# Quantised groups in pieces, constant matrix products in other places, and five quantisations one slot later, in a two-layer transformer kernel

## The reference

```python
# layer 0
h = layernorm(x) * (1 + ca) + sa
Qr, Kr = rotate(h @ Wq.T), rotate(h @ Wk.T)
x = x + ga * softmax(where(mask, Qr @ Kr.T / sqrt(128), -inf)) @ (h @ Wv.T)
h = layernorm(x) * (1 + cb) + sb
gate, y = fp4(h) @ fp4(w_gate).T, fp4(h) @ fp4(w_up).T          # 352 columns
x = x + gb * (fp4(silu(gate) * y) @ fp4(w_down).T)
# layer 1, other rows of modulation
h = layernorm(x) * (1 + ca) + sa
x = x + ga * softmax(causal(h @ qk @ h.T / sqrt(128))) @ h @ ov
h = layernorm(x) * (1 + cb) + sb
x = x + gb * (top2_experts(h) + shared_expert(h))
```

## Time and profile before

| | us |
|---|---|
| median of three runs | 714.09 (713.89 to 716.97) |
| the profiled execution | 714.27 |
| its span, from the first to the last instruction | 712.4 |
| TensorE busy in matrix products | 625.6 (88%), 3764 instructions |
| VectorE busy | 479.4 (67%), 1270 |
| ScalarE busy | 339.9 (48%), 693 |
| GpSimd busy | 226.1 (32%), 248 |
| granted TensorE clock, mean over the span | 0.978 |

### The profile page before, as it was taken

One profiled execution on the slowest core, in us unless ns is written; L12 is line 12 of the kernel. 1 busy time (PEld: TensorE's weight loads), 2 busy tenths in 40 slices (PEclk: granted clock), 3 DMA queues, 4 the chain that ended last, 5 costly groups with the idle time before them and its releaser, 6 DMA issues.

```text
span 712.4 us, 10866 instructions
## 1 busy us (share of the span) xinstructions
PE 625.6 (88%) x3764; PEld 486.2 (68%) x3782; DVE 479.4 (67%) x1270; ACT 339.9 (48%) x693; POOL 226.1 (32%) x248
## 2 busy tenths in 40 slices
PE   5888898988779989988899889868889996998996
PEld 4356687877556778775678777746668874676774
DVE  5966499786777557627569886687545436775665
ACT  1133454565535464443445465534655553554553
POOL 3424645453644301005456454474310002000000
PEclk9989999999999999999999999989999999999999
DMA  8200000000000000000000000100000000001011
GB/s 248 81 1 1 1 2 1 1 1 1 1 0 1 2 1 1 1 2 1 1 1 1 1 1 1 52 5 1 1 1 1 1 1 1 0 16 29 16 30 30
DMA packets 12173, 9.64 MB, mean 14 GB/s; under 512 B 1804, under 2 KB 10840, under 8 KB 12120
## 3 DMA queue, kind: packets, MB, share of 16 engines
q1 hardware_dynamic: 12120, 8.95, 4.2%
HBM read 6.84 MB, written 2.10 MB: 13 GB/s over the span
## 4 chain that ended last, share of the span: by engine, by line
PE 58%; DVE 21%; ACT 8%; POOL 7%; issue 5%; DMA 1%; SPq 0%; ACTq 0%; POOLq 0%; DVEq 0%
PE ps L819 12%; PE ps L687 10%; PE ps L797 7%; PE ps L968 4%; PE ps L970 4%; PE ps L969 4%; PE ps L646 3%; ACT xn L1087 2%; PE ps L842 2%; PE ps L707 2%; PE ps L843 2%; POOL rstd L516 2%; PE ps L858 2%; DVE row_max L1410 1%; DVE ha L1455 1%
## 5 line engine op out<-in xcount | busy, mean ns | idle before, releaser
L1147 ACT ACTIVATE probsT<-ps 128x512 f32<-128x512 f32 (+3 forms) x160 | 85.2, 533 | 162.8 <-PE ps L797 162.8
L819 PE MATMUL ps<-v_sb,probsT 128*128 128x129 f32 (+1 forms) x1124 | 151.4, 279 | 3.7 <-ACT probsT L1149 3.7
L819 PEld LDWEIGHTS ps<-v_sb,probsT 128*128 128x128 f32 (+1 forms) x1124 | 137.6, 191 | 8.8 <-ACT probsT L1149 5.5
L1410 DVE TENSOR_REDUCE row_max<-ps 128x1 f32<-128x512 f32 (+2 forms) x144 | 87.7, 620 | 54.4 <-PE ps L687 25.7
L797 PE MATMUL ps<-ident,probs 128*128 128x128 f32 (+1 forms) x562 | 90.8, 278 | 15.2 <-ACT hT L1077 7.8
L1121 ACT ACTIVATE probs<-ps,neg_max 128x512 f32<-128x512 f32 (+7 forms) x158 | 93.1, 620 | 17.9 <-DVE neg_max L1417 14.1
L797 PEld LDWEIGHTS ps<-ident,probs 128*128 128x128 f32 (+1 forms) x562 | 64.4, 140 | 46.0 <-issue 42.1
L545 POOL TENSOR_TENSOR hq<-ha,hp 128x352 f32<-128x352 f32 x32 | 29.9, 934 | 118.3 <-DVE hp L1460 118.3
L1222 ACT ACTIVATE probs<-ps 128x512 f32<-128x512 f32 x40 | 24.0, 599 | 44.8 <-PE ps L970 44.8
L687 PE MATMUL ps<-k_high,q_high 128*128 128x512 f32 (+5 forms) x100 | 42.1, 421 | 2.8 <-ACT probs L1121 2.2
L515 POOL TENSOR_SCALAR minus_mean<-mv 128x4 f32<-128x4 f32 (+1 forms) x16 | 3.8, 238 | 122.7 <-DVE veps L1278 122.5
(11 more groups left out here) (245 smaller groups left out, 1372.7 us busy)
## 6 DMA issues: line engine op xcount, KB each, us to landing
out<-x_sb SPq DMA_DIRECT2D x8, 256.0 KB, 2.3
x_sb<-in_L_attn_x SPq DMA_DIRECT2D x2, 512.0 KB, 6.5
hT_all<-in_L_wmod SPq DMA_DIRECT2D x2, 384.0 KB
rope_cos<-table_cos SPq DMA_DIRECT2D x1, 768.0 KB, 8.1
rope_sin<-table_sin SPq DMA_DIRECT2D x1, 768.0 KB, 10.1
rope_cos<-table_cos SPq DMA_DIRECT2D x1, 256.0 KB, 4.5
rope_sin<-table_sin SPq DMA_DIRECT2D x1, 256.0 KB, 6.2
moe_raw<-in_L_ffn_expert_gate_w SPq DMA_DIRECT2D x1, 256.0 KB, 2.7
```

The source lines that it names most:

```text
L819: mm = pe.matmul(bank(OUT_AT, 0, V_W), probsT[0:size, n % 4, k * P:(k + 1) * P], v_sb[0:size, j, :], start=(c == 0 and k == 0), stop=(c == ...
L1147: ins = act.activation(probsT[:, n % 4, 0:full], bank(TURN, 0, full), ACT.Copy)
L1410: ins = dve.tensor_reduce(dst, ps[:, start:start + width], AX.X, ALU.max, negate=single)
```

## The change

- `modulate_1` works tile by tile: eight instructions of 128 columns for two of 512, and ScalarE signals every normalised tile.
- `xq_scaled`, the transposition and the copy of a group work in two parts (`FP4_PARTS`): the first tile, then the other three. TensorE transposes the first tile in slot 4g + 6 and the others in slot 4g + 7.
- `grid_slot(n)` is the slot in which tile n is quantised: n + 6 as before, but n + 7 for tiles 10 to 14 (`GRID_LATE`). Of these, 10 to 13 are quantised by VectorE ahead of the next tile's gating, and 14 at tile 15's place, ahead of it. The transposition of these tiles stays where it was.
- The constant products in `WAITS_AT_HEAD` go. New are some inside `turn_group`, behind the wait for the bank and ahead of the wait for the input (`WAITED_FOR`: 3 for norm0's groups 1 to 3; 2, 8, 10 and 5 for norm2's four), three ahead of each of the keys' projections in slots 0, 2 and 4, 11 or 18 for the 9 at the end of a batch and 4 behind them, and 10 ahead of the sums over the experts' choices. In batch 0 that is 20 products more, in batch 1 27 more.
- From slot 4 on the rounding of rotated keys and queries stands at the end of a slot on ScalarE (L1156) and behind `modulate_1` and `hq_scaled` on GpSimd (L575).

```diff
 SLOTS = 2 * TILES
+FP4_PARTS = ((0, 1), (1, GROUP))
 FFN_LAG, DOWN_LAG = 6, 8
-
-
-WAITS_AT_HEAD = {FFN_LAG: 11, TILES + 1: 8, TILES + 5: 10}
+GRID_LATE = range(TILES - FFN_LAG, TILES - 1)
+
+
+WAITED_FOR = {**{("norm0", g): 3 for g in range(1, GROUPS)}, ("norm2", 0): 2, ("norm2", 1): 8, ("norm2", 2): 10, ("norm2", 3): 5}
+
+
+def grid_slot(n):
+
+    return n + FFN_LAG + (n in GRID_LATE)
 
...
-    firsts = (("fp4_in", FFN_LAG), ("norm2", DOWN_LAG + GROUP + 1), ("norm3", TILES + GROUP + 2))
+    firsts = (("fp4_first", FFN_LAG), ("fp4_rest", FFN_LAG + 1), ("norm2", DOWN_LAG + GROUP + 1), ("norm3", TILES + GROUP + 2))
     turns = [(kind, group_at(slot, first)) for kind, first in firsts if group_at(slot, first) is not None]
...
-                    pool.wait_ge(h_step, b * 2 * GROUPS + 2 * g + 1)
-                    pool.tensor_tensor(h, h, row(0), ALU.add).then_inc(h_step, 1)
+                    tiles = [xn[:, g, t * P:(t + 1) * P] for t in range(GROUP)]
+                    first = b * TILES + g * GROUP
+
+                    def add_shift(t):
+                        pool.wait_ge(h_scaled, first + t + 1)
+                        pool.tensor_tensor(tiles[t], tiles[t], mod_row_now[:, 0, :], ALU.add).then_inc(h_shifted, 1)
+
+                    for t in range(GROUP):
+                        pool.wait_ge(xn1_ready, first + t + 1)
+                        pool.tensor_tensor(tiles[t], tiles[t], mod_row_now[:, 1, :], ALU.mult).then_inc(h_scaled, 1)
+                        if t:
+                            add_shift(t - 1)
+                    add_shift(GROUP - 1)
...
-                    pool.tensor_tensor(xq[:], qa[:], qp[:], ALU.add).then_inc(xq_step, 1)
-                    pool.wait_ge(xq_step, b * 2 * GROUPS + 2 * g + 1)
-                    pool.tensor_tensor(xq[:], xq[:], qp[:], ALU.subtract).then_inc(xq_step, 1)
-                    pool.wait_ge(xq_step, b * 2 * GROUPS + 2 * g + 2)
-                    blocks = xq[:].rearrange("p (k e) -> p k e", e=BLOCK)
-                    pool.tensor_tensor(blocks, blocks, qs[:, 2, :].unsqueeze(2).to_broadcast(
-                        [P, GROUP * P // BLOCK, BLOCK]), ALU.mult).then_inc(xq_ready, 1)
+                        pool.wait_ge(turned, TURN_AT[b, "fp4_rest", g - 1] + 1)
+                    for part, (a, z) in enumerate(FP4_PARTS):
+                        cols, done = slice(a * P, z * P), b * 4 * GROUPS + 4 * g + 2 * part
+                        pool.tensor_tensor(xq[:, cols], qa[:, cols], qp[:, cols], ALU.add).then_inc(xq_step, 1)
+                        pool.wait_ge(xq_step, done + 1)
+                        pool.tensor_tensor(xq[:, cols], xq[:, cols], qp[:, cols], ALU.subtract).then_inc(xq_step, 1)
+                        pool.wait_ge(xq_step, done + 2)
+                        by_block = xq[:, cols].rearrange("p (k e) -> p k e", e=BLOCK)
+                        scales = qs[:, 2, a * P // BLOCK:z * P // BLOCK].unsqueeze(2)
+                        pool.tensor_tensor(by_block, by_block, scales.to_broadcast([P, (z - a) * P // BLOCK, BLOCK]),
+                                           ALU.mult).then_inc(xq_ready, 1)
...
 
-                for s in range(SLOTS):
-                    at = lambda first: group_at(s, first)
+                def rope_lows(s):
                     if early_group(s, K0_SLOT + 1) is not None:
                         rope_low(early_group(s, K0_SLOT + 1), 0)
...
+                    at = lambda first: group_at(s, first)
+                    if s < FP4_SLOT:
...
                     if at(NORM1_SLOT + 1) is not None:
                         modulate_1(at(NORM1_SLOT + 1))
-                    if ffn_tile(s, FFN_LAG) is not None:
-                        hq_scaled(s - FFN_LAG)
+                    for n in (s - FFN_LAG - 1, s - FFN_LAG):
+                        if 0 <= n < TILES and s == grid_slot(n):
...
+                            hq_scaled(n)
+                    if s >= FP4_SLOT:
...
                 def turn_group(key):
 
                     kind, g = key
-                    if kind == "fp4_in":
-                        pe.wait_ge(xq_ready, b * GROUPS + g + 1)
+                    if kind in ("fp4_first", "fp4_rest"):
+                        part = int(kind == "fp4_rest")
+                        pe.wait_ge(xq_ready, 2 * (b * GROUPS + g) + part + 1)
                         bank_free(key)
-                        for t in range(GROUP):
+                        for t in range(*FP4_PARTS[part]):
                             mm = pe.transpose(bank(TURN, t * P, (t + 1) * P), xq[:, t * P:(t + 1) * P], ident[:])
                         mm.then_inc(turned, 1)
                         return
+                    bank_free(key)
+                    keep_clock(TURN, WAITED_FOR.get(key, 0))
                     if kind in ("norm0", "next"):
                         pe.wait_ge(xn0_ready, b * GROUPS + g + 1 + (GROUPS if kind == "next" else 0))
                     else:
                         pe.wait_ge(xn_ready, b * len(XN_AT) + XN_AT[key] + 1)
-                    bank_free(key)
                     turn_normed(g)
 
...
+                        keep_clock(3, 3)
                         out_of_bank(("norm0", k))
...
                     g, t = divmod(n, GROUP)
-                    if t == 0:
-                        out_of_bank(("fp4_in", g))
+                    if t < 2:
+                        out_of_bank((("fp4_first", "fp4_rest")[t], g))
...
                     n = len(turn_chunks(*divmod(s, TILES)))
-                    if s in WAITS_AT_HEAD:
...
                     first_values_and_scores(b, b + 1)
-                keep_clock(GATE, 9)
+                keep_clock(GATE, 11 if b + 1 < BATCH else 18)
                 turn_group(("norm3", GROUPS - 1))
+                keep_clock(GATE, 4)
...
                     mm.then_inc(unsel_turned, 1)
+            pe.wait_ge(unselT_ready, 1)
+            keep_clock(0, 10)
...
-                    if kind == "fp4_in":
-                        act.activation(xqT[:], bank(TURN), ACT.Copy).then_inc(copied, 1)
+                    if kind in ("fp4_first", "fp4_rest"):
+                        a, z = FP4_PARTS[kind == "fp4_rest"]
+                        act.activation(xqT[:, a * P:z * P], bank(TURN, a * P, z * P), ACT.Copy).then_inc(copied, 1)
                         return
...
+                def normalise(kind, t, g):
+
+                    return act.activation(xn[:, g, t * P:(t + 1) * P], x_sb[:, b * TILES + g * GROUP + t, :], ACT.Identity,
+                                          scale=rstd[:, kind, t:t + 1], bias=shift[:, kind, t:t + 1])
...
-                def normalise_1(g):
-                    normalise(0, g, g).then_inc(xn1_ready, 1)
+                        normalise(0, t, g).then_inc(xn1_ready, 1)
...
-                    if early_group(s, K0_SLOT + 1) is not None:
-                        round_rope(early_group(s, K0_SLOT + 1), 0)
-                    if early_group(s, Q0_SLOT + 1) is not None:
-                        round_rope(early_group(s, Q0_SLOT + 1), 1)
+                    if s < FP4_SLOT:
+                        round_ropes(s)
...
+                    if s >= FP4_SLOT:
+                        round_ropes(s)
...
                         if g:
-                            dve.wait_ge(xq_ready, b * GROUPS + g)
-
-                    dve.wait_ge(h_step, b * 2 * GROUPS + 2 * g + 2)
+                            dve.wait_ge(xq_ready, 2 * (b * GROUPS + g))
+
+                    dve.wait_ge(h_shifted, b * TILES + (g + 1) * GROUP)
...
+
+                def ahead(n):
+
+                    return n in GRID_LATE[:-1]
 
...
+                    if ahead(s - FFN_LAG - 1):
+                        quantise_h(s - FFN_LAG - 1)
                     if ffn_tile(s, FFN_LAG) is not None:
                         combine(s - FFN_LAG)
...
-                    if ffn_tile(s, FFN_LAG) is not None:
-                        quantise_h(s - FFN_LAG)
+                    for n in (s - FFN_LAG - 1, s - FFN_LAG):
+                        if 0 <= n < TILES and s == grid_slot(n) and not ahead(n):
+                            quantise_h(n)
```

29 lines of the change are left out of this document (16 added, 13 removed).

## The result

The changed kernel takes 708.23 us (median; 707.41 to 708.97), the kernel before 715.42 on the same chips: ratio 0.990, 95% interval 0.988 to 0.992, so 1.0% faster. The profiled execution has a span of 705.6 us where that of before has 712.4: 6.8 us less. Forecast were 702, in a range from 694 to 709. The direction and the range hold, but of the 12.4 us that the sum named 6.9 came.

The account below looks back on a forecast made before the run. TensorE, busy 88% of the span, was taken as the bound, so time falls by less waiting or a higher clock. Terms summed to -12.4 us from 714.3, giving 701.9, forecast as 702; the 8-in-10 range was 694 to 709.

Parts of the forecast that it names:

- group 0: Slot 6: first tile of xq and the values' copy come earlier; gate and up start 1.9 us sooner per batch.
- group 1: Slot 10: 0.7 us from the pieces, 0.9 from VectorE being held less beside them; 1.6 us won per batch.
- group 3: Slot 18 on: late quantisation removes the 3.84 us wait; 3.1 us won in batch 0, 4.5 in batch 1.
- second parts: Later copy of a group's other three tiles: hidden beside score products except in slot 15, +0.3 us per batch.
- constant products: Slots 0 and 4: added products that waits do not hide cost 2.9 us over both batches.
- clock in slot 25: Batch 1, near 532 us: the stretch at half clock goes, 1.3 us won.
- Rival 3: GpSimd's modulation pieces are slow, 0.79 us each; each modulation ends 2.5 us later; 711 us, chance 0.09.
- VectorE sets the pace: Behind slot 18: VectorE, 15.0 of 16 us busy, can win only its idle time in slot 18, 2.44 to 3.7 us.
- Rival 1: Double quantisation in slot 21 delays finishing tile 21; TensorE waits there and in slots 19, 20; 708 us, chance 0.22.
- Rival 4: Late quantisation also frees slot 19's statistics and norm2's group 2, so more is won; 694 to 698 us, chance 0.14.
- Rival 2: Slots 17 to 20: quantisation ahead of the gated product holds the gate bank; 728 us; with milder forms, chance 0.06.
- signs of being wrong: Waits over 1 us for gated product or hq; constant product before ready input; first xq tile over 1.8 us after quantisation.

Follow-up runs that it names:

- the third: Rounding of rotated keys and queries back at its old place in all slots, against the changed kernel; 713.43 us, ratio 0.997 to the kernel before.
- the seventh experiment: Each input group finished, transposed and copied in one part, against the changed kernel; 710.70 us, ratio 0.993 to the kernel before.
- the sixth experiment: GpSimd's modulation as two products of 512 columns again, against the changed kernel; 712.55 us, ratio 0.995 to the kernel before.
- The kernel with four edits: Changed kernel without constant products in slots 0, 2, 4, 21; old rounding place up to slot 4; tile 14 quantised behind normalisation, 15 in slot 22; 700.56 us.

## Why the prediction was right in direction and range, and 6 us off

| term | predicted, both batches | measured by slots |
|---|---|---|
| group 0 (slots 5, 6) | -3.8 | -1.61 -1.85 = -3.46 |
| group 1 (slot 10) | -3.2 | -1.56 -1.60 = -3.16 |
| group 3 (slots 18 to 23) | -7.6 | -1.33 -2.72 = -4.05 |
| second parts (slots 7, 11, 15) | +0.6 | +1.77 +1.76 = +3.53 |
| constant products (slots 0, 4) | +2.9 | +0.28 +1.34 = +1.62 |
| clock in slot 25 | -1.3 | -1.36 |
| sum | -12.4 | -6.9 |

Of the 5.5 us that are missing, 3.6 are in group 3 and 2.9 in the second parts; the constant products cost 1.3 less than their term. Two rows are not firm: the -0.16 us that slot 0 of batch 0 gives to the constant products lies inside what that slot varies by, and the clock in slot 25 need not be the change's doing, for the late quantisation alone, with the constant products of the kernel before, has 8.80 us there too.

- *Price of a piece.* Predicted 0.47, 0.47 and 0.4 us. The changed kernel's lines (count, busy us, mean ns, idle before):

```profile
L551 POOL TENSOR_TENSOR xn<-xn,mod_row_now 128x128 f32<-128x128 f32 x32 | 15.0, 479 | 4.6 <-ACT xn L1115 4.6
...
L574 POOL TENSOR_TENSOR xq<-qa,qp 128x128 f32<-128x128 f32 x8 | 3.6, 455 | 16.3 <-DVE qp L1498 16.3
...
L580 POOL TENSOR_TENSOR xq<-xq,qs 128x128 f32<-128x128 f32 x8 | 3.2, 402 | 0.6
```

  That is 0.455 to 0.479 and 0.402. Rival 3 falls.
- *Group 0.* The sum was right, in part by luck (at full clock slot 6 gave 2.4 us where 1.9 were forecast, and slot 5 took back 0.5 that the sum did not have), and its reason half of it. I credited the pieces with the first tile and took the freed copy as its follower; the third and the seventh experiment show that neither gives anything without the other. And I did not see that the same move puts 0.61 us ahead of the exponentials in slot 4.
- *Group 1.* Right, part by part: the pieces of `xq` were put at 0.7 us and give 0.86 (11.47 against 10.61 with the modulation whole). That VectorE is held less beside short pieces was put at 0.9 us; it is 0.70.
- *Slot 18.* It named what is late next, the gated product at 196.8, 2.5 us behind the end of slot 17 at 194.31, costing 1.5 to 2. It came at 195.67, again 2.5 us behind that end (193.17), and TensorE waited 1.67. But the whole 3.84 us was credited to the late quantisation. Alone it removes half; alone the pieces remove all but 0.76.
- *Behind slot 18: the step that failed.* "VectorE sets the pace" was taken to mean that nothing is paid later. In slots 19 to 23 2.5 us a batch are paid: 0.5 for the second part of group 3, 0.5 in slot 20, 1.9 and 0.3 in slots 22 and 23 by the late quantisation (9.26 and 6.65 us without it), of which the one buffer for two quantisations in slot 21 accounts for 1.2, less 0.6 in slot 21. Where the other 1.0 us of slots 22 and 23 comes from no run isolates; TensorE still waits there for the scaled tile. Rival 1 had this place, the double quantisation in slot 21, and its total, 708, is the measured time. That agreement is luck in part: its 3.5 us for group 3 is near the 4.05, but it had 1.4 for slot 10, where 3.16 came, and nothing for slots 7 and 11, which cost 1.9; and the wait for `qh` was not named.
- *The constant products of slot 21.* The prediction kept them as before. With the statistics of slot 19 no longer behind tile 13 (Rival 4's mechanism) the input came earlier, and 1.6 us of that gain went into products that had nothing left to cover. The text named the sign of it, a constant product ahead of an input that is ready, but did not work it out.
- *The second part of a group.* "Hidden" was wrong: TensorE does three transpositions that stand alone, at 0.45 to 0.83 us, where in slot 14 they had cost nothing.
- *Rival 2* was wrong in size: the quantisation ahead of the gated product costs TensorE 1.67 us in slot 18, nothing in slot 19 and 0.74 in slot 20 (6.50 against 5.76 us without it).
- *What would show it.* The wait for `xq` went from 11.9 to nothing and the clock at slot 18 is 1.00, as forecast. VectorE's wait for the tanh fell to 24.9 only and not under 20. All but the last of the signs of being wrong came: waits of over 1 us for the gated product (1.7) and for `hq` (1.5), and constant products ahead of an input that was ready. The first of them was at odds with the prediction's own working, which had put 1.5 to 2 us there.

The Trainium skill (SBUF — State Buffer, section "SBUF: two separate sides") says that of VectorE and GpSimd the one that starts first has their shared port pair for its whole instruction and blocks the other, where VectorE's instruction has two inputs in SBUF or runs in a two-port mode. The runs agree: beside GpSimd's products of 1.27 us two of VectorE's instructions take 1.30 and 1.32 us (the sixth experiment), in the changed kernel, with products of 0.48 us, 0.48 each, and slot 10 is 0.70 us longer.

## What to carry to other kernels

Ask of an input that comes earlier what else stands between it and its user on each in-order queue: here the early tile was worth nothing until a rounding had left the queue of another engine, and the freed queue nothing until the tile came early. Filler work belongs to a wait, so whenever an edit moves an input, time each filler against the new readiness. And when work is put off so that two of a kind fall into one slot, look at the buffer between the engines first: one copy made VectorE stand 2.6 us.

## What the runs showed of the hardware that was not expected

Ahead of the scores at 75.35 us TensorE stands 1.61 us in the kernels that round behind the normalisation there, and in 6 of 16 such places (eight kernels with that order, two batches each) the granted clock is 1.2 GHz for 3.4 us from within 1.4 us behind it; of the 12 places where it stands 1.09 us (six kernels) none has it. The same code in the same kernel has it in one batch and not in the other. It costs little here: 0.23 us over slots 5 and 6.

Elsewhere such a stretch costs more. The kernel before and the one with the late quantisation alone have the same code in slot 0 of batch 1 and in slot 25: only the second has a stretch of 3.4 us at 1.2 GHz in the former (13.40 against 11.77 us), only the first has one in the latter, in batch 1 (10.15 against 8.80). The kernel with four edits has executions at a mean clock of 1.000 (698.5 to 699.3 us) and at 0.987 to 0.989 (701.9 to 703.2); of the second kind there is no profile, so where its clock falls is open.
